# Copying every gather of expert results into spare slices and adding on VectorE

## What is computed

```python
x = x + attn_a(layernorm(x))     # causal attention, 16 heads of 8, with rotary positions
x = x + ffn(layernorm(x))        # mixture of experts, "layer 0" of the kernel
x = x + attn_b(layernorm(x))     # one head of 128, scores outside a band of 64 are set to 0
x = x + ffn(layernorm(x))        # the same experts again, "layer 1" of the kernel

def ffn(x):                      # 4096 tokens, 64 experts of width 128
    sel_val, sel_idx = top_k(sigmoid(x @ expert_sel.T), 4)
    out = sum over the four chosen experts k of (relu(x @ keys[k]) * sel_val) @ values[k]
```

## Time and profile before

| | |
|---|---|
| runs, median | 1199.96 us |
| profiled execution, span | 1216.6 us |
| PE busy | 818.3 us (67%) |
| POOL busy | 876.4 us (72%) |
| DVE busy | 728.4 us (60%) |
| ACT busy | 560.2 us (46%) |
| indirect DMAs that add to x_res | 176, busy 274.1 us |
| indirect DMAs that copy results | 80, busy 75.6 us |
| chain that ended last | PE 37%, POOL 23%, DVE 15%, issue 14%, ACT 6% |

### The profile page before, as it was taken

How to read it: one execution, slowest core, us unless ns; L and a number is a source line. 1 busy time by engine, 2 the same in 40 slices (tenths; PEclk the granted TensorE clock), 3 DMA queues, 4 the chain that set the end, 5 groups by cost and what they waited for, 6 DMA issues and landing times.

```text
span 1216.6 us, 22596 instructions
## 1 busy us (share of the span) xinstructions
PE 818.3 (67%) x7290; PEld 601.3 (49%) x7290; DVE 728.4 (60%) x2057; ACT 560.2 (46%) x1505; POOL 876.4 (72%) x934
## 2 busy tenths in 40 slices
PE   1899978888688766697898665454458874991000
PEld 0444444443344325697898644343357774991000
DVE  3787988888878424764667846566256772661111
ACT  1177666676566743564565413333126552661000
POOL 6345667879767675887888878878727578887776
PEclk9789999999999986898999866567679897996555
DMA  6556544533272332599898412212325564994222
GB/s 182 171 181 210 191 159 172 171 99 105 75 232 58 96 95 76 144 264 215 176 215 177 81 44 42 39 46 37 100 72 162 149 183 127 263 273 106 69 63 63
DMA packets 226258, 163.80 MB, mean 135 GB/s; under 512 B 15968, under 2 KB 213600, under 8 KB 226144
## 3 DMA queue, kind: packets, MB, share of 16 engines
q1 hardware_dynamic: 183968, 110.43, 31.7%
q0 software_dynamic: 36096, 33.59, 13.8%
q10 hardware_dynamic: 6080, 18.35, 4.1%
HBM read 78.94 MB, written 83.36 MB: 133 GB/s over the span
## 4 chain that ended last, share of the span: by engine, by line
PE 37%; POOL 23%; DVE 15%; issue 14%; ACT 6%; another core or an unknown queue 3%; DMA 3%; ACTq 0%; POOLq 0%; DVEq 0%; SPq 0%
POOL x_res L1743 7%; PE ps L771 6%; PE ps L780 5%; PE ps L672 5%; POOL sorted_rows L1727 4%; POOL v_aug L1745 3%; PE ps L631 3%; PE ps L760 3%; POOL x_scaled L1745 2%; ACT arena L978 2%; DMA x_res<-result_rows,dest 2%; DVE row_max L1211 2%; PE ps L689 2%; POOL arena L1776 1%
## 5 line engine op out<-in xcount | busy, mean ns | idle before, releaser
L1743 POOL DMA_INDIRECT x_res<-result_rows,dest x176 | 274.1, 1557 | 60.6 <-issue 48.8
L978 ACT ACTIVATE arena<-ps 128x512 f32<-128x512 f32 x320 | 182.8, 599 | 79.9 <-PE ps L604 75.1
L1727 POOL DMA_INDIRECT sorted_rows<-v_aug,dest x144 | 139.7, 970 | 83.7 <-issue 33.8
L1410 DVE COPY arena<-ps 128x512 f32<-128x512 f32 x128 | 88.2, 689 | 132.0 <-PE ps L760 71.7
L771 PE MATMUL ps<-arena 128*128 128x128 f32 x1024 | 147.2, 290 | 23.0 <-DVE arena L1410 11.5
L631 PE MATMUL ps<-arena 64*128 64x128 bf16 (+3 forms) x576 | 130.2, 305 | 28.9 <-DMA arena<-k_parts 15.1
L771 PEld LDWEIGHTS ps<-arena 128*128 128x128 f32 x1024 | 134.4, 205 | 26.9 <-issue 13.9
L1211 DVE TENSOR_REDUCE row_max<-ps 128x1 f32<-128x512 f32 (+1 forms) x192 | 127.0, 682 | 33.6 <-PE ps L651 31.9
L967 ACT COPY arena<-ps 128x512 f32<-128x512 f32 x128 | 75.0, 586 | 145.6 <-PE ps L780 117.0
L780 PE MATMUL ps<-arena 128*128 x1024 | 140.1, 281 | 0.9 <-ACT arena L967 0.9
L1727 POOL DMA_INDIRECT sorted_rows<-x_scaled,dest x112 | 111.5, 995 | 35.9 <-issue 24.6
(11 more groups left out here) (207 smaller groups left out, 1649.5 us busy)
## 6 DMA issues: line engine op xcount, KB each, us to landing
arena<-sorted_rows SPq DMA_DIRECT2D x128, 256.0 KB
result_rows<-arena SPq DMA_DIRECT2D x128, 256.0 KB
sorted_rows<-arena ACTq DMA_DIRECT2D x16, 1024.0 KB, 4.6
arena<-q_parts SPq DMA_DIRECT2D x16, 512.0 KB, 4.0
arena<-k_parts SPq DMA_DIRECT2D x16, 512.0 KB, 5.0
q_parts<-parts SPq DMA_DIRECT2D x52, 128.0 KB, 2.8
k_parts<-parts SPq DMA_DIRECT2D x38, 128.0 KB, 3.0
x_res<-result_rows,dest POOLq DMA_INDIRECT x176
```

The lines of the kernel that those rows point to most:

```text
L978: nc.scalar.activation(prob[:, grp % 2, pr % 2, PROB_AT[u]:PROB_AT[u] + T], ps[:, v % 2, :], ACT.Exp, scale=SCALE_A).then_inc(exp_done, 1)
L1410: nc.vector.tensor_copy(xtt[:, n % 2, :], ps[:, e_bank(0, layer, half, n), :]).then_inc(t1_done, 1)
L1727: g.indirect_dma_start(sorted_d[b // HALF][:, :], bass.IndirectOffsetOnAxis(dest[:, 16 * b + n:16 * b + n + 1], 0), scaled_rows(layer, b)[ ...
L1743: g.indirect_dma_start(x[:, TT * b + t, :], None, rows, index, compute_op=ALU.add).then_inc(lane, 16)
```

## The change

Every gather is now a copy into a 2 KB slice (512 float32 for each partition), and every add is made by DVE, `added` counting them in order. The slices come from x_scaled, both halves of v_aug, and tiles that are free by then (`w_attn`, a third of `parts`, `max_t` made larger, a piece of the arena, the head outputs, the rope tiles). Layer 0 alternates between two sets of four slices, so the gather of batch b waits, slice by slice, for DVE's adds of batch b-2; layer 1 has seven sets. DVE's layer-0 adds of batch b stand in iteration b-2, one after each of places 4, 5, 8 and 10 (batch 0: all four ahead of the loop). DVE's layer-1 adds stand inside the last expert pass, one after every second step from step 8 (13 of 32), and the rest at the end. POOL's gathers of layer 0's batches 5, 6 and 7 move ahead by one place: gathers 4 and 5 in iteration 1, gather 6 after scatter 0 of layer 1, gather 7 after scatter 1. The memset after the scatters of layer 1's batches 5 to 7 goes to xn0 (512 columns) instead of w_attn (640).

```diff
-PLAIN = tuple((1, b) for b in range(3, B))
+ADD_FROM, ADD_EACH = 8, 2
...
+def gathers_ahead(it):
+    return {-1: (2,), 0: (3,), 1: (4, 5)}.get(it, ())
+def gathers_behind(it):
+    return {2: (6,), 3: (7,)}.get(it, ())
+def added_count(layer, b, c):
+    return TOPK * (B * layer + b) + c + 1
...
+        def slice_freed(layer, b, c):
+            if layer == 0:
+                return added_count(0, b - 2, c) if b >= 2 else 0
+            before = {0: (0, B - 2), 3: (0, B - 1), 7: (1, 0)}
+            return added_count(*before[b], c) if b in before else 0
...
-            def add_rows(layer, b):
-                xb = x[:, TT * b:TT * b + TT, :]
-                for c in range(TOPK):
-                    for lane in landed:
-                        dve.wait_ge(lane, landed_count("gather", layer, b) - 16 * (TOPK - 1 - c))
-                    if c:
-                        dve.wait_ge(added, TOPK * PLAIN.index((layer, b)) + c)
-                    nc.vector.tensor_tensor(xb, xb, gathered_rows(layer, b)[:, TT * c:TT * c + TT, :], ALU.add).then_inc(added, 1)
+            def add_rows(layer, b, c):
+                xb = x[:, TT * b:TT * b + TT, :].rearrange("p t n -> p (t n)")
+                for lane in landed:
+                    dve.wait_ge(lane, landed_count("gather", layer, b) - 16 * (TOPK - 1 - c))
+                if c:
+                    dve.wait_ge(added, added_count(layer, b, c - 1))
+                nc.vector.tensor_tensor(xb, xb, gathered_slice(layer, b, c), ALU.add).then_inc(added, 1)
+            def add_soon(b, c):
+                if b < B:
+                    add_rows(0, b, c)
...
             dve.wait_ge(band_made, BANDS)
+            for c in range(TOPK):
+                add_rows(0, 0, c)
...
+                add_soon(b + 2, 0)
                 beside(b, 5)
                 if route:
                     choice = choose(B + r, *evacuated("LG", r))
                     advance(choice, 3)
+                add_soon(b + 2, 1)
                 beside(b, 6)
...
+                add_soon(b + 2, 2)
                 beside(b, 9)
...
                     advance(place_rows, 6)
+                add_soon(b + 2, 3)
                 beside(b, 11)
...
+            soon = [(b, c) for b in range(B) for c in range(TOPK)]
             for s in range(STEPS):
                 expert_step(1, 1, s)
-            for b in range(B):
-                if (1, b) in PLAIN:
-                    add_rows(1, b)
+                if s >= ADD_FROM and (s - ADD_FROM) % ADD_EACH == 0:
+                    add_rows(1, *soon.pop(0))
+            for b, c in soon:
+                add_rows(1, b, c)
...
                 for c in range(TOPK):
+                    if slice_freed(layer, b, c):
+                        pool.wait_ge(added, slice_freed(layer, b, c))
                     for t in range(TT):
                         lane = next_lane()
                         at = 16 * b + TOPK * t + c
-                        if adding:
-                            g.indirect_dma_start(x[:, TT * b + t, :], None, rows, index, compute_op=ALU.add).then_inc(lane, 16)
-                        else:
-                            g.indirect_dma_start(gathered_rows(layer, b)[:, TT * c + t, :], None, rows, index).then_inc(lane, 16)
+                        g.indirect_dma_start(gathered_slice(layer, b, c)[:, P * t:P * t + P], None, rows,
+                                             bass.IndirectOffsetOnAxis(dest[:, at:at + 1], 0)).then_inc(lane, 16)
...
             gather(0, 0)
+            pool.wait_ge(parts_out, 192 * B)
+            for i in range(2):
+                pool.wait_ge(mrow_out[i], 16 * B)
             gather(0, 1)
             for b in range(-1, LAST_IT_B + 1):
-                far, late = b + 3, b - 2
-                if b <= 1:
+                late = b - 2
+                for far in gathers_ahead(b):
                     gather(0, far)
...
                         if late >= PACED_FROM:
-                            rest()
-                if 1 < b < B - 3:
+                            rest(xn0[:, :, :])
+                for far in gathers_behind(b):
                     gather(0, far)
```

More of the change, by code:

```diff
@@ L156, in transfer_order @@
     for b in range(-1, LAST_IT_B + 1):
-        far, late = b + 3, b - 2
-        if b <= 1:
-            out.append(("gather", 0, far))
+        out += [("gather", 0, far) for far in gathers_ahead(b)]
+        late = b - 2
         if 0 <= late < B:
             out.append(("scatter", 1, late))
-        if 1 < b < B - 3:
-            out.append(("gather", 0, far))
+        out += [("gather", 0, far) for far in gathers_behind(b)]
     return out + [("gather", 1, b) for b in range(B)]
@@ L411, in scaled_rows, with four_slices, gathered_slice @@
             return xs_b[:, b % 2] if layer or b == B - 1 else xs_a
[L413 to L427, removed]
+        def four_slices(rows):
+            return [rows[:, TT * c:TT * c + TT, :].rearrange("p t n -> p (t n)") for c in range(TOPK)]
+        spare = [w[:, 0:T], parts[:, 2].rearrange("p n t -> p (n t)").bitcast(F32),
+                 max_room[:, :, :].rearrange("p n t -> p (n t)").bitcast(F32), arena[:, 9504:9504 + T]]
+        heads = [ytf[:, i, :] for i in range(8)]
+        ropes = [qt[0], qt[1], kt[0], kt[1]]
+        first_homes = (four_slices(xs_a), spare)
+        second_homes = (four_slices(xs_a), four_slices(xs_b[:, 0]), four_slices(xs_b[:, 1]), spare, heads[0:4], heads[4:8], ropes)
+        def gathered_slice(layer, b, c):
+            homes = second_homes if layer else first_homes
+            return homes[b % len(homes)][c]
+        def slice_freed(layer, b, c):
[3 more added lines that the diff above has]
+            return added_count(*before[b], c) if b in before else 0
         def scaled_in(it, k):
@@ L575, in _ @@
             for b in range(B):
-                if (1, b) not in PLAIN:
-                    for lane in landed:
-                        sp.wait_ge(lane, landed_count("gather", 1, b))
-                else:
-                    sp.wait_ge(added, TOPK * (PLAIN.index((1, b)) + 1))
+                sp.wait_ge(added, added_count(1, b, TOPK - 1))
                 sp.dma_start(out_d.rearrange("(t p) c -> p t c", p=P)[:, TT * b:TT * b + TT, :],
@@ L1585, in combined_stats @@
             def combined_stats(b):
[L1586 to L1591, removed]
+                dve.wait_ge(added, added_count(0, b, TOPK - 1))
                 finish(ln_stats(x[:, TT * b:TT * b + TT, :], st0, mv0, rs0, b, ln2))
@@ L1707, in _, with rest @@
             transfers, rests = count(), count(1)
-            def rest():
+            def rest(room):
                 n = next(rests)
@@ L1713, in rest @@
                     pool.wait_ge(rested, n - 1)
-                g.memset(w[:, :], 0.0).then_inc(rested, 1)
+                g.memset(room, 0.0).then_inc(rested, 1)
             def next_lane():
@@ L1733, in gather @@
                     pool.wait_ge(y_sent[u], 16 * uses(group_number(layer, b // HALF, groups_holding(b)), u))
-                adding = (layer, b) not in PLAIN
-                if not adding and last_reader(layer, b):
-                    pool.wait_ge(added, last_reader(layer, b))
+                rows = result_d[layer][b // HALF][0:G * P * groups_holding(b), :]
                 for c in range(TOPK):
+                    if slice_freed(layer, b, c):
+                        pool.wait_ge(added, slice_freed(layer, b, c))
                     for t in range(TT):
@@ L1813, in _ @@
                         if it >= B + 1:
-                            rest()
+                            rest(w[:, :])
             pool.wait_ge(pv_done, 4 * B)
```

6 lines of the change are left out of this document (2 added, 4 removed).

## The result

The changed kernel takes 1132.28 us (median of 4 runs, 1128.23 to 1139.86), the kernel before beside it 1197.93 (4 runs): ratio 0.9465, 95% interval 0.9431 to 0.9499. A later, longer comparison gave 1130.54 (6 runs) and 0.9438 (0.9404 to 0.9472). The forecast was 1150, own range 1130 to 1170; the gain is 65.6 us where 50 were forecast. The profiled execution took 1139.86 us with a span of 1137.9, some 7 us above the median.

What follows compares the result with a forecast made beforehand. The prediction took POOL's gather issue, above all the adding gathers, as the largest bound, in stage three and less visibly stage two. From 1200 us: -25 - 1.7 - 13.7 - 16 + 6 = -50, giving 1150 us, range 1130 to 1170.

Steps and rivals of the forecast that it cites:

- Stage three, -25: Layer 1's gathers: 48 adding gathers become copies, -30.3 us, less 5 us for landing waits.
- that for landings, +5: Stage three's 48 copies beside the last expert pass wait for earlier transfers to land: 5 us, bounds 0 and 19.
- the rival on landings: All 48 copies beside the expert pass go at 1.65 us each: 14 us more, 1164 us; chance 0.06.
- The adds beside POOL: Stage three's 32 DVE adds of 0.69 us are covered by POOL's issuing and cost 0.
- The rival priced at 22 us: Shared-port lock: each of stage three's 32 adds holds POOL for 0.69 us, 1172 us; chance 0.03.
- The pauses, -1.7: Smaller memset after scatters; only batch 7's 16 are on the path: 0 to -2 us, taken as -1.7.
- PE's idle, -13.7: Stage two: scatter 3 lands before PE asks for layer 1's expert loads, so PE's idle of 13.67 us goes.
- DVE's iterations, -16: Stage two: iterations 2, 3 and 5 could shorten to iteration 4's length; bounds 0 and -32, middle taken.
- the base of 1200: Changes set against 1200 us, taking the profiled span of 1216.6 as lengthened by two "remote" DVE idles, 14.3 us.
- Stage two's adds, +6: Layer 0's 32 DVE adds, 22 us in all, mostly covered by DVE's waits: +6 us, bounds 0 and 25.
- Stage three alone: Stage two's idles, tied to dense scatter bursts, and adds eat its 13.7 us gain: 1175 us; chance 0.20.
- The slower case: Dense copies disturb PE, ACT and DVE by 12 us in each of six batches: 1238 us; chance 0.06.

Runs made afterwards that it cites:

- e5: Changed kernel with four indirect transfers in flight instead of three: 1119.42 us, ratio 0.9335.
- e1: Kernel before, adding gathers kept, only gathers 5 to 7 of layer 0 moved one place earlier: 1194.93 us, ratio 1.0001.
- e3: Changed kernel, but layer 1's batches 0 to 2 add again in the gather and DVE adds batches 3 to 7 after the pass: 1152.92 us.
- e12: Changed kernel run and profiled again, unaltered: 1130.54 us, ratio 0.9438.
- e2: Changed kernel, but layer 0's gathers add again in the old order, so only layer 1's all copy: 1177.86 us, ratio 0.9844.
- e8: Changed kernel with layer 0's 32 DVE adds cut to one column of 512: 1127.56 us, ratio 0.9425.
- e6: Changed kernel with layer 0's gather 7 moved behind scatter 3, its adds to just before batch 7's statistics: 1137.68 us, ratio 0.9504.
- e4: Changed kernel with gathers 5 to 7 of layer 0 back in their old places: 1148.87 us, ratio 0.9641.
- e7: Changed kernel without the pauses after the 16 scatters of the last batch: 1128.43 us, ratio 0.9442.
- e9: Kernel before with four indirect transfers in flight instead of three: 1188.94 us, ratio 0.9943.

## Why the prediction was right, and where it was wrong

The direction was right, the adding gather was the price in both stages, and the time, 1132, lies in the range. It lies 2 us from its lower end, and partly by luck, for two errors stood against each other: stage three was forecast 7 us too high, stage two 25 us too low. Stage two's 50 us are more than the 46 that the prediction's best corner gave it (2 + 13.7 + 32 - 2).

*Stage three, -25.* 13.5 us by the two profiles, 17 to 19 by the undisturbed ones. The mis-sized term is that for landings, +5: the 48 copies took 75.3 us where the sum had 60.1 for them without waits, so it was about 15, near the upper bound of 19 that the prediction had worked out. e5 takes 11.5 of these away (75.3 to 63.8) and shows the mechanism. That stage three still gave 17 to 19 has a second reason: the 48 adding gathers took 92.7 and 92.9 us in e1 and e3, not 90.4. The mistake was to take few waits of adding gathers, which leave a landing 4.0 us, as a sign that few take longer than 2.8. This is also the rival on landings: its mechanism held, at 1.57 us in place of 1.65. It had 0.06.

*The adds beside POOL.* Cost nothing in stage three: the copies of the tail are 1.27 us apart, those of the earlier trace rows were 1.25, both with a DVE add every 5 us beside them. In the tail before, the 19 steps that an add overlaps average 1.25 us and the 60 others 1.25; in the changed kernel 1.29 and 1.27, in e12 1.26 and 1.27. The rival priced at 22 us the exclusive lock that the Trainium skill ("SBUF — State Buffer", the shared port pair) describes; no run here shows it between such adds and the issue of indirect transfers. The same page, under "Who interferes with whom", reports that `tensor_tensor` did not stall such a DMA, and the trace agrees.

*The pauses, -1.7.* The memset took 542 ns, near the proportional bound: 16 x 0.11 = 1.7.

*PE's idle, -13.7, and DVE's iterations, -16.* Together -30, and with the adds' +6 and the pauses stage two was to give 25 us; it gave 316.8 - 267 = 50 (329.3 - 266.5 = 63 against the disturbed profile of before). The step that failed is "late next is DVE's chain of iterations, not POOL", with its reading of the iterations. The profiled execution was disturbed for longer than I allowed: the base of 1200 took 14.3 us as accident, but it is 24 us over e1's span of 1192.8, and about as much over what the 17-run median of 1194.95 gives; some 12 us of them lie ahead of the first mark and 13 in stage two. DVE, held up, came late to its gathers and so waited only 1.24 us for gather 7. In e2, whose stage two is the same and undisturbed, it waits 23.10 and 25.79 us: 49 us, about the whole gain. The marks agree. In e2 scatter 3 starts 158.0 us behind the first mark, in the changed kernel 109.2 (e12: 109.0), and from there to the first layer-1 gather are 158.8 and 157.3. POOL's timeline of e2:

```profile
837.67 1.03 POOL L1746 DMA_INDIRECT sorted_rows<-v_aug,dest  x1 [0.30 <-issue]
```

The iterations of 28 us had nothing to give back, and the gate was not one idle of 13.67 but everything POOL issues between scatter 0 and scatter 3. The prediction had that sum nearly right as a time (scatter 3 landed at 822; SP's loads came at 821.16) and then credited only 13.7 of the 50 us between 871.62 and there, for the rest seemed covered by DVE. A slip stands in the reading of the earlier trace rows too: the idle of 0.93 at 798.25 lies ahead of the cast at 806.57 that ends iteration 4, so it is iteration 4's and not, as the prediction has it, iteration 5's, and says nothing on how long iteration 5 had to be.

*Stage two's adds, +6.* About 4 (e8).

*The signs.* Scatter 3 at 800 to 810: 798.60. No idle before PE's first layer-1 transposes: wrong, 4.14 us on PE and 10.78 on DVE; e6 shows that it can be had only for another wait. Iterations of 31 to 34 us: 28.6 to 29.9. Of the signs of error one came, copies 1.6 us apart beside the pass. POOL did idle on `added`, 8.38 and 5.79 us, but ahead of gathers 4 and 5, and scatter 0 still started 1.1 us behind its indices. Idles of 10 us on several engines between 544 and 696 did not come.

*The rivals.* Stage three alone: refuted by e2 and e3, it holds about a quarter of the gain. The slower case, dense copies that cost the engines over 6 us a batch: the first indices came at 679 to 683 in kernels with copies and without (e1, e2 against e4, e7), though 80 to 96 copies lie ahead of them. Beside the last pass they cost at most a few us: it ends 82.2 us behind the first copy in the changed kernel, and 79.2 to 81.5 behind the first adding gather in before, e1, e3 and e9.

## What to carry to other kernels

Where an engine issues without a pause between two points that others wait for, count what it issues there: that bounds the gain to be had, even if the profiled execution shows the waiting engine late for reasons of its own. Before a stall is called short, ask whether the profile is disturbed ahead of it; the profile of a near variant tells it.

When a queue's entries get cheaper to issue, the limit on how many are in flight tightens with it (here from 4.0 to 2.8 us of time to land): raise it in the same step. A place in the queue has no worth of its own; the same move was worth 0 us with slow entries and 17 to 19 us with fast ones.

## What the runs showed of the hardware

An indirect gather that adds does not only take 1557 ns to issue where a copy takes 944. The software queue's packets, 36096 in the kernel before for 33.59 MB and 16384 here for the same bytes, give 2 KB a packet for copies; with 32 packets a copy, the 176 adding gathers took the other 36096 - 336 x 32 = 25344, 144 each, about 455 bytes a packet. Two other mixtures bear this out to the packet: e2 with 128 adding gathers has 30720 = 128 x 144 + 384 x 32, and e3 with 48 has 21760 = 48 x 144 + 464 x 32. In the 75 us behind the first gather of stage three the kernel before moves 246 GB/s at a DMA share of 1.03 with 40 adding gathers, the changed one 247 GB/s at 0.89 with 48 copies.

With four of these 64 KB copies in flight in place of three, beside an expert pass at 250 GB/s, PE was not slowed (68.22 and 67.48 us busy of 75, pass over 82.2 and 81.8 us behind the first copy). With three, a copy had on average 3 x 1.57 - 0.95 = 3.8 us to land, and POOL idled 22.3 us for landings, so many used them.
